# Intermediate tensors of an image kernel laid out in DRAM with the row parity outermost

## What is computed

```python
x = x + _L0_conv_ref(_gn(x), L0_conv_kernel, L0_conv_bias, L0_conv_W)   # 3x3 conv, then 64x64
x = x + _L1_conv_ref(_gn(x), ...)   # deformable conv: 18 bilinear samples per pixel (9 taps, 2 groups)
x = x + _L2_conv_ref(_gn(x), ...)   # focal modulation
x = x + _L3_conv_ref(_gn(x), ...)   # triangle product
```

```python
# L2, focal modulation
y = einsum('bhwc,cd->bhwd', x, Wf) + bf
q, ctx, gates = y[..., :C], y[..., C:2*C], y[..., 2*C:]        # gates: 4 channels
for l, k in enumerate((k0, k1, k2)):                            # depthwise 3x3, 5x5, 7x7
    ctx = gelu(dwconv_same(ctx, k))
    ctx_all = ctx_all + ctx * gates[..., l:l + 1]
ctx_all = ctx_all + gelu(mean(ctx, axis=(1, 2))) * gates[..., 3:]
x_out = layernorm(q * (ctx_all @ Wh + bh)) * gamma + beta
x_out = x_out @ Wp + bp
# L3, triangle
a, b, g = (sigmoid(einsum('bijc,dc->bijd', zn, Wx)) for Wx in (Wa, Wb, Wg))
sum_k = einsum('bikc,bkjc->bijc', a, b)                         # a 128x128x128 product per channel
return g * einsum('bijc,dc->bijd', layernorm(sum_k), Wf)
```

## Time and profile before

| | |
|---|---|
| median of 3 runs | 12509.48 us (12509.34 to 12513.1) |
| the profiled execution | 12486.59 us, its span 12484.8 us, granted TensorE clock 0.770 |
| POOL busy | 8772.3 us (70%), of it 8747.9 in L451 |
| PE busy / DVE busy / ACT busy | 7830.9 (63%) / 5278.9 (42%) / 1730.9 (14%) |
| DMA | 1314.96 MB, 105 GB/s; queue q1 (SP) 16.4%, q0 (the gathers) 18.5% of 16 engines' span |

### The profile page before, as it was taken

How to read it: one execution, slowest core, us unless ns; L and a number is a source line. 1 busy time by engine, 2 the same in 40 slices (tenths; PEclk the granted TensorE clock), 3 DMA queues, 4 the chain that set the end, 5 groups by cost and what they waited for, 6 DMA issues and landing times.

```text
span 12484.8 us, 135272 instructions
## 1 busy us (share of the span) xinstructions
PE 7830.9 (63%) x46082; PEld 6363.4 (51%) x46082; DVE 5278.9 (42%) x6338; ACT 1730.9 (14%) x3045; POOL 8772.3 (70%) x9269
## 2 busy tenths in 40 slices
PE   4766667666467765554457775555457776655487
PEld 3554445545457644444446754444446754444373
DVE  3344444444344444343344444443344444344333
ACT  1001101011011112110011112210011111310025
POOL 2777777777777777777777777777777777777600
PEclk7877778777688877776678877776678887777698
DMA  3333434334244423432234422332225432342274
GB/s 108 84 105 103 129 90 129 112 98 126 71 127 155 133 66 80 112 94 61 71 98 168 143 70 73 101 104 70 56 81 173 141 97 64 92 115 79 62 246 129
DMA packets 1033592, 1314.96 MB, mean 105 GB/s; under 512 B 186528, under 2 KB 831328, under 8 KB 1015968
## 3 DMA queue, kind: packets, MB, share of 16 engines
q0 software_dynamic: 294912, 604.57, 18.5%
q1 hardware_dynamic: 661664, 657.15, 16.4%
q10 hardware_dynamic: 76800, 50.34, 1.3%
HBM read 1082.07 MB, written 292.16 MB: 110 GB/s over the span
## 4 chain that ended last, share of the span: by engine, by line
POOL 68%; issue 23%; PE 4%; DVE 1%; DMA 1%; ACT 0%; SPq 0%; POOLq 0%; PEld 0%; DVEq 0%; ACTq 0%; PEldq 0%
POOL gat L451 68%; PE stage L984 2%; PE stage L887 1%; DVE srow L1433 0%; DMA gat<-table,idx 0%; DMA table<-room 0%; PE acc L887 0%; DVE gat L1426 0%; DMA room<-b_d 0%; POOLq L449 0%; PE pt L887 0%; PE wtb L887 0%; PEld acc L1091 0%; PE stage L939 0%; POOLq L447 0%
## 5 line engine op out<-in xcount | busy, mean ns | idle before, releaser
L451 POOL DMA_INDIRECT gat<-table,idx x9216 | 8747.9, 949 | 3008.0 <-issue 2803.2
L1091 PE MATMUL acc<-stt,wk 128*128 128x128 f32 (+1 forms) x30600 | 4364.2, 307 | 228.7 <-ACT stt L862 228.7
L1091 PEld LDWEIGHTS acc<-stt,wk 128*128 128x128 f32 (+1 forms) x30600 | 4212.4, 221 | 539.7 <-ACT stt L862 337.5
L1080 PE MATMUL pt<-mat,srow 128*128 128x128 f32 x2048 | 509.5, 396 | 3746.8 <-DVE srow L1433 3746.4
L1080 PEld LDWEIGHTS pt<-mat,srow 128*128 128x128 f32 x2048 | 329.5, 197 | 3948.8 <-DVE srow L1433 3935.0
L1402 DVE COPY idx<-idxn 128x18 uint32<-128x18 uint32 x512 | 97.6, 191 | 5230.6 <-DMA gat<-table,idx 5222.5
L1433 DVE TENSOR_REDUCE srow<-gat 128x576 f32<-128x2304 f32 x512 | 2081.1, 4065 | 0.3
L1426 DVE TENSOR_TENSOR gat<-gat,wtb 128x2304 f32<-128x2304 f32 x512 | 1306.2, 2551 | 62.9 <-DMA gat<-table,idx 62.5
L887 PE MATMUL stage<-room,mat 128*128 128x512 f32 (+1 forms) x1696 | 1000.0, 721 | 350.1 <-DVE room L1307 67.9
L862 ACT ACTIVATE stt<-pt 128x512 f32<-128x512 f32 x512 | 305.6, 597 | 5980.9 <-PE pt L1080 5968.4
L984 PE MATMUL stage<-room 128*128 128x128 f32 x7680 | 890.2, 278 | 20.5 <-DMA room<-toep 18.4
(11 more groups left out here) (179 smaller groups left out, 3854.6 us busy)
## 6 DMA issues: line engine op xcount, KB each, us to landing
gat<-table,idx POOLq DMA_INDIRECT x9216
room<-toep SPq DMA_DIRECT2D x64, 1792.0 KB, 18.4
room<-toep SPq DMA_DIRECT2D x64, 1280.0 KB, 11.7
table<-room SPq DMA_DIRECT2D x128, 512.0 KB
room<-toep SPq DMA_DIRECT2D x64, 768.0 KB, 5.3
toep<-in_taps SPq DMA_DIRECT2D x128, 224.0 KB
toep<-in_taps SPq DMA_DIRECT2D x128, 160.0 KB
room<-in_x SPq DMA_DIRECT2D x4, 4096.0 KB, 14.4
```

The source lines that it names most:

```text
L451: nc.gpsimd.indirect_dma_start(gat[r][:, k % K9 * G + k // K9, :], None, table[b][0:NENT * ENTRY].rearrange("(n e) -> n e", e=ENTRY), bass ...
L1080: ins = nc.tensor.transpose(pt[:, m, :], srow[r % 2][:, m * P:(m + 1) * P], M["ident"])
L1091: ins = nc.tensor.matmul(acc[a][:, 0:W], wk[0:kk, m, dx, block_at * C:block_at * C + P], stt[s][0:kk, m, dx:dx + W], start=start and m == ...
```

## The change

The six tensors lie in DRAM as [image, parity, channel, row of that parity, column]. On the channel side a tile is then one DMA over all 128 partitions, each moving 4 x 128 contiguous numbers. On the row side a group is two DMAs, one for each parity, into every second partition. Waits and limits on the DMA semaphores change with the number of DMAs. No arithmetic changes, and no step moves in the programs of PE, DVE or POOL.

```diff
-        ctxd = dram("ctxd", [NB, C, H, W])
+        ctxd = dram("ctxd", [NB, 2, C, HP, W])       # and so gated, mixd, a_d, b_d, s_d
...
-        def planes(d, b, t, par):
-            return d[b].rearrange("c (h r) w -> r c h w", r=2)[par, :, ds(4 * t, 4), :]
-        def half(a, par, n=C):
-            return a[par * n:(par + 1) * n, :].rearrange("c (h w) -> c h w", w=W)
-        def group(d, b, q):
-            return d[b, ds(QC * q, QC), :, :].rearrange("c h w -> h c w")
+        def planes(d, b, t):
+            return d[b].rearrange("r c h w -> (r c) h w")[:, ds(4 * t, 4), :]
+        def rows(a):
+            return a.rearrange("p (h w) -> p h w", w=W)
+        def group(d, b, q, par):
+            return d[b, par, ds(QC * q, QC), :, :].rearrange("c h w -> h c w")
...  context, SP
-                        for par in range(2):
-                            sp.dma_start(planes(ctxd, b, t, par), half(cs[u], par)).then_inc(cx_out[u], 16)
+                        sp.dma_start(planes(ctxd, b, t), rows(cs[u])).then_inc(cx_out[u], 16)
                         sp.wait_ge(gate_s, n + 2)
-                        for par in range(2):
-                            sp.dma_start(planes(gated, b, t, par), half(gs[u], par, 4)).then_inc(cx_out[u], 16)
+                        sp.dma_start(planes(gated, b, t), rows(gs[u][0:8, :])).then_inc(cx_out[u], 16)
...  depthwise, SP
-                    sp.dma_start(gates, gated[b].rearrange("l h w -> h l w")).then_inc(gates_in, 16)
+                    for par in range(2):
+                        sp.dma_start(gates[par:P:2], gated[b, par].rearrange("l h w -> h l w")).then_inc(gates_in, 16)
...
-                                sp.dma_start(cin[0][u][:, :, CPAD:CPAD + W], group(ctxd, b, q))\
-                                    .then_inc(ctx_in[u], 16)
+                                for par in range(2):
+                                    sp.dma_start(cin[0][u][par:P:2, :, CPAD:CPAD + W], group(ctxd, b, q, par))\
+                                        .then_inc(ctx_in[u], 16)
...  modulate, SP (close and s_d in the same way)
-                        for par in range(2):
-                            sp.dma_start(half(ca[u], par), planes(mixd, b, t, par)).then_inc(ca_in[u], 16)
+                        sp.dma_start(rows(ca[u]), planes(mixd, b, t)).then_inc(ca_in[u], 16)
...  operands, SP
-                            for par in range(2):
-                                sp.dma_start(planes(dst, b, t, par), half(src[u], par)).then_inc(abg_out[u], 16)
+                            sp.dma_start(planes(dst, b, t), rows(src[u])).then_inc(abg_out[u], 16)
...  triangle, SP
-                        sp.dma_start(ta[u], group(a_d, b, q)).then_inc(ab_in[u], 16)
-                        sp.dma_start(tb[u], group(b_d, b, q)).then_inc(ab_in[u], 16)
+                        for src, dst in ((a_d, ta), (b_d, tb)):
+                            for par in range(2):
+                                sp.dma_start(dst[u][par:P:2], group(src, b, q, par)).then_inc(ab_in[u], 16)
...  depthwise, ACT (triangle and s_d in the same way)
-                        act.dma_start(group(mixd, b, 2 * i + u), mix[u]).then_inc(mix_out[u], 16)
+                        for par in range(2):
+                            act.dma_start(group(mixd, b, 2 * i + u, par), mix[u][par:P:2]).then_inc(mix_out[u], 16)
```

More of the change, by code:

```diff
@@ L190, in build @@
         toep = [dram(f"toep{l}", [C // QC, H, QC, k * H]) for l, k in enumerate(TAPS)]
-        ctxd = dram("ctxd", [NB, C, H, W])
[L192 to L195, removed]
+        ctxd = dram("ctxd", [NB, 2, C, HP, W])
+        gated = dram("gated", [NB, 2, 4, HP, W])
+        mixd = dram("mixd", [NB, 2, C, HP, W])
+        a_d = dram("a_d", [NB, 2, C, HP, W])
+        b_d = dram("b_d", [NB, 2, C, HP, W])
         g_d = dram("g_d", [P, NB * IMG])
-        s_d = dram("s_d", [NB, C, H, W])
+        s_d = dram("s_d", [NB, 2, C, HP, W])
         mat = sb("mat", [P, len(MATS), P])
@@ L570, in depthwise_end @@
                     for u in range(2):
-                        sp.wait_ge(mix_out[u], 16 * IT * (b + 1) + 1)
+                        sp.wait_ge(mix_out[u], 32 * IT * (b + 1) + 1)
                 def modulate(b, i):
@@ L597, in operands_end @@
                     for u in range(flight(b)):
-                        sp.wait_ge(abg_out[u], 80 * round_of(b, TB // flight(b), u) + 1)
+                        sp.wait_ge(abg_out[u], 48 * round_of(b, TB // flight(b), u) + 1)
                 def triangle(b, i):
@@ L617, in close @@
                         sp.wait_ge(c_cen_p, n + 1)
-                        for par in range(2):
-                            sp.dma_start(half(ss[u], par), planes(s_d, b, t, par)).then_inc(s_in[u], 16)
+                        sp.dma_start(rows(ss[u]), planes(s_d, b, t)).then_inc(s_in[u], 16)
                     for u in range(flight(b)):
@@ L746, in context @@
                         act.wait_ge(gate_p, b * TB + flight(b) * i + u + 1 + flight(b))
-                        act.wait_ge(cx_out[u], 64 * round_of(b, i, u) + 1)
+                        act.wait_ge(cx_out[u], 32 * round_of(b, i, u) + 1)
                         nc.scalar.activation(gs[u][0:8, :], banks[2 * u + 1][0:8, :], ACT.Identity, bias=b_gate)\
@@ L820, in operands @@
                     for u in range(flight(b)):
-                        act.wait_ge(abg_out[u], 80 * round_of(b, i, u) + 1)
+                        act.wait_ge(abg_out[u], 48 * round_of(b, i, u) + 1)
                         for k, (bank, dst, bias) in enumerate(((2 * u + 1, sa, ba), (2 * u, sB, bb))):
@@ L834, in triangle @@
                         act.wait_ge(prod, q + 1 + flight(b))
-                        act.wait_ge(s_out[u], 16 * round_of(b, i, u) + 1)
+                        act.wait_ge(s_out[u], 32 * round_of(b, i, u) + 1)
                         nc.scalar.activation(so[u], banks[2 * u + 1].rearrange("p (c w) -> p c w", w=W), ACT.Copy)\
@@ L838, in triangle @@
                         act.wait_ge(so_s, q + 1 + flight(b))
-                        act.dma_start(group(s_d, b, flight(b) * i + u), so[u]).then_inc(s_out[u], 16)
+                        for par in range(2):
+                            act.dma_start(group(s_d, b, flight(b) * i + u, par), so[u][par:P:2]).then_inc(s_out[u], 16)
                 def close(b, i):
@@ L975, in depthwise @@
                             if l == 0:
-                                pe.wait_ge(ctx_in[u], 16 * j + 16)
+                                pe.wait_ge(ctx_in[u], 32 * j + 32)
                                 pe.wait_ge(padded_c, b + 1)
@@ L1000, in modulate @@
                         mm(banks[2 * u], M["wq"], xm[u]).then_inc(q_p, 1)
-                        pe.wait_ge(ca_in[u], 32 * (round_of(b, i, u) + 1))
+                        pe.wait_ge(ca_in[u], 16 * (round_of(b, i, u) + 1))
                         pe.wait_ge(m_added, n(u) + 1)
@@ L1042, in triangle @@
                         q = b * TB + flight(b) * i + u
-                        pe.wait_ge(ab_in[u], 32 * (round_of(b, i, u) + 1))
+                        pe.wait_ge(ab_in[u], 64 * (round_of(b, i, u) + 1))
                         pe.wait_ge(aT_s, q + 1)
@@ L1060, in close @@
                     for u in range(flight(b)):
-                        pe.wait_ge(s_in[u], 32 * (round_of(b, i, u) + 1))
+                        pe.wait_ge(s_in[u], 16 * (round_of(b, i, u) + 1))
                         pe.wait_ge(c_y_s, n(u) + 1)
@@ L1258, in context @@
                         dve.wait_ge(ctx_p, n + 1)
-                        dve.wait_ge(cx_out[u], 64 * round_of(b, i, u) + 1)
+                        dve.wait_ge(cx_out[u], 32 * round_of(b, i, u) + 1)
                         ts(cs[u], banks[2 * u], V["b_ctx"], None, ALU.add).then_inc(ctx_s, 1)
@@ L1267, in depthwise_begin @@
                     ins.then_inc(padded_c, 1)
-                    dve.wait_ge(gates_in, 16 * (b + 1))
+                    dve.wait_ge(gates_in, 32 * (b + 1))
                 def depthwise(b, i):
@@ L1283, in depthwise @@
                         dve.wait_ge(gelu_s[u], 3 * j + 2)
-                        dve.wait_ge(mix_out[u], 16 * j + 1)
+                        dve.wait_ge(mix_out[u], 32 * j + 1)
                         then(u, tt(mix[u], cin[1][u][:, :, CPAD:CPAD + W], gate(0), ALU.mult), 1)
```

4 lines of the change are left out of this document (2 added, 2 removed).

## The result

The kernel after takes 12524.12 us (median of 20 runs, 12519.08 to 12530.66), the kernel before 12507.34 us (20 runs, 12502.44 to 12513.1). The ratio is 1.0014, with a 95% interval of 1.0008 to 1.0020. The change makes the kernel slower by 0.14%, about 17 us, where the forecast was 4 us faster.

What follows compares the result with a forecast made beforehand. The prediction took POOL's gathers to bound the kernel until 11795.5 us, unchanged, with only the later stages moving. Their terms sum to -3.7 us, from 12509.5 to 12505.8 us; the range was 12485 to 12526.

Steps and rivals of the forecast that it cites:

- The frame: Whole kernel: POOL's gathers set the time up to 11795.5 us; the change adds 0 there, bounds -6 and +8 us.
- last gather starts within 8 us of 11795.5: Sign expected in the changed profile: POOL's gather distance stays 1.254 us, so its last gather hardly moves.
- End of context: Context stage: SP issues fewer stores and keeps up, so the last ctxd store lands earlier, -7.1 us.
- Start of depthwise: Before depthwise's first band SP has four DMAs instead of two: +0.5 us, bounds 0 and +1.9.
- Store of mixd: End of depthwise: ACT issues four DMAs instead of two for the last two groups, +1.1 us (0 to +1.6).
- End of operands and modulate: SP's fewer stores let the last g_d store start earlier, -7.4 us; one mixd load per tile starts modulate earlier, -1.0.
- Triangle and store of s_d: Triangle: SP's 16 loads per iteration delay the last, +10.3 us; ACT's extra s_d issues add +3.3 us.
- The form's price: Row-side DMAs of 64x4x128 occupy their issuer about 0.62 us, taken from the trace with contiguous partitions.
- the upper bound: Triangle's loads cost at most +16 us: 0.85 for each DMA and a slower clock of a longer waiting PE.
- Start of close: Close: four s_d loads instead of eight land earlier, and PE gives part back, -3.4 us.
- the +8 us kept for the gathers: Upper allowance in the range for POOL's gather distance growing before 11795.5 us; the forecast itself took 0.
- the rivals: Triangle bound by transfers, 12491, chance 0.18; gathers' depthwise excess gone, 12477, 0.04; loads into every second partition dearer, 12543, 0.05.

Runs made afterwards that it cites:

- the second pair: Kernels before and after, both unchanged, traced once more on another chip; one execution took 12488.72 us before and 12504.53 us after.

## Why the prediction was wrong

- *The frame.* POOL's gathers set the time up to 11.8 ms and the change does not touch them: right, 11554 to 11560 us in eight traces of different layouts on chips of the usual speed, and the one 11577.4 belongs to no layout. By it the prediction's sign "last gather starts within 8 us of 11795.5" failed in the first trace (11817.7) and held in the second (11794.7).
- *End of context*, -7.1: measured -7.1 and -7.6. *Start of depthwise*, +0.5: -0.1 and +1.1 in the two pairs of traces.
- *Store of mixd*, +1.1: measured +17.6 and +18.7 for the piece. **This is the step that failed.** The prediction counted ACT's new issues once, for the last pair of groups, and of the other seven iterations it said that "the 28.7 us iterations of depthwise are PE's own". The chain named only PE there, since ACT was a few tenths of a us early. The prediction did not ask what stood behind the stores in ACT's program: the gelu that PE's second layer waits for. Four issues of 0.64 us in place of two of 0.39, with their register work 3.68 - 1.83 = 1.85 us more, took the slack and then PE's time: from one second layer to the next 3.0 us four times, and 1.4 to 1.5 us at either end, where the 192 products take 21.72 us and not 23.35. That the slower stretch would stop covering for ACT, 1.6 of the 3.0 us, was in no sum either.
- *End of operands and modulate*, -8.4: -10.0 and -7.5.
- *Triangle and store of s_d*, +13.6: +16.3 and +15.4. The form's price was right. From SP's first issue to the last turn it is 14.5 us in the first iteration, as forecast, and 14.8 to 15.0 in the others. An iteration takes 17.5 to 18 us instead of the 17.5 that the sum had. The slower clock that the upper bound allowed for hardly showed: over the piece PE's granted clock was 0.68 before and 0.67 after, its busy time 35.9 and 36.5 us.
- *Start of close*, -3.4: -2.7 and +0.1, at the edge of what two traces agree on.

Without the failed step the sum measured in the first pair of traces is 14.9 - 16.5 = -1.6 us, near the -3.7 that was forecast; in the second pair it is 19.7 - 17.6 = +2.1 us, so even the sign of the rest is not settled. The time lies within the range, on the wrong side of the kernel before, and that is luck: for the stages the range had +7 us at most, and 15 to 20 came; what took it in was the +8 us kept for the gathers, which did not move, and a median of the kernel before that was 2 us lower in twenty runs than in three. None of the rivals was this one: all three put the danger in the triangle's loads or the gathers, none on ACT.

## What to carry to other kernels

When an edit adds DMA issues to a compute engine, read the program of that engine behind them, in every iteration of the loop and not only at its end: the next thing in the queue may be what the busy engine waits for. A chain that names one engine alone does not say how early the others were; that has to be read from the idle time at each hand-over. An issue has a price by its form, and a layout that halves the issues on the side where they stand on the path and doubles them on a side in the loop moves the time instead of saving it; keep the layout by tensor, not for all.

## What the runs showed of the hardware

- A DMA of 64 partitions with four pieces of 512 bytes in each kept its issuer busy for 0.62 to 0.64 us in the median, with neighbouring partitions or every second, as load or store, on SP or ACT (only the loads of the gates took 0.67). Over 32 partitions it was 0.34 as a store of `s_d` and 0.43 as a load of the gates, over 128 partitions 0.39 to 0.46 with four pieces and 0.34 to 0.36 with one.
- Behind a pause of the same 2.2 us TensorE's granted clock over the next 5.6 us was 0.70 in one turn and 1.00 in another, and 48 products took 7.0 and 5.6 us. Work of another engine that hid behind the slower stretch no longer does when the stretch falls elsewhere.
- The median gather was 944 ns in one execution of the same kernel and 947 in another, which is 22 us of the whole. A difference of nearly 0.2% between two single profiles of this kernel can be that alone.
- One chip ran every version at 18.5 ms, with the gathers' own 944 to 947 ns unchanged and some 320 pauses between them, about 6 ms in sum. From the load of x on, the pieces behind the last gather agreed with those of the same two kernels on another chip to within 3 us each.
